# Conditional residual kernel: weight loads in runs of 2 KB with strided transposes, a smaller bias part, and row loads moved to ScalarE

## The reference

```
x: (128, 64, 256) fp32      cat_ids: (128,) in 0..63
W: (64, 256, 256) fp32      b: (64, 256) fp32
out = x + einsum('bsd,bdh->bsh', x, W[cat_ids]) + b[cat_ids][:, None, :]
```

## Time and profile before

| what | us |
|---|---|
| median of 3 runs | 99.18 |
| lowest, highest | 98.57, 100.05 |
| profiled execution, its own time | 99.0 |
| profiled execution, span | 97.0 |
| TensorE busy | 85.5 (88%) |
| VectorE, ScalarE, GpSimd busy | 53.6, 55.1, 34.3 |

### The profile page before, as it was taken

How to read it: one execution, slowest core, us unless ns; L and a number is a source line. 1 busy time by engine, 2 the same in 40 slices (tenths; PEclk the granted TensorE clock), 3 DMA queues, 4 the chain that set the end, 5 groups by cost and what they waited for, 6 DMA issues and landing times.

```text
span 97.0 us, 3027 instructions
## 1 busy us (share of the span) xinstructions
PE 85.5 (88%) x788; PEld 58.1 (60%) x788; DVE 53.6 (55%) x130; ACT 55.1 (57%) x98; POOL 34.3 (35%) x65
## 2 busy tenths in 40 slices
PE   0318969999998699999999999999999999999980
PEld 0107735676666466666767575868666866676640
DVE  2792407648236275748575475655187519664840
ACT  1402284692537282985866760977278827885500
POOL 5400000000000028999969623939702493000000
PEclk9999999999999999999999999999999999999999
DMA  0899999999999999998999999999996679999563
GB/s 13 261 345 365 348 349 346 350 346 349 350 347 349 348 350 325 341 356 267 402 367 402 365 400 370 388 388 367 329 355 252 220 171 392 409 372 343 170 209 108
DMA packets 19970, 31.25 MB, mean 322 GB/s; under 512 B 1521, under 2 KB 15986, under 8 KB 19954
## 3 DMA queue, kind: packets, MB, share of 16 engines
q0 software_dynamic: 4640, 16.26, 46.6%
q1 hardware_dynamic: 13602, 13.18, 42.3%
q10 hardware_dynamic: 1712, 1.64, 5.2%
HBM read 25.30 MB, written 8.39 MB: 347 GB/s over the span
## 4 chain that ended last, share of the span: by engine, by line
PE 62%; ACT 1%; DVE 0%; issue 0%; ACTq 0%; SPq 0%
PE mm_ps L598 42%; PE xt_ps L507 11%; PE mm_ps L584 6%; PE xt_ps L598 2%; ACT w_slot L337 1%; DVE rows L477 0%; PE xt_ps L584 0%; ACTq L337 0%; SPq L208 0%
## 5 line engine op out<-in xcount | busy, mean ns | idle before, releaser
L598 PE MATMUL mm_ps<-w_slot,xT 128*64 128x256 f32 x496 | 57.1, 380 | 2.1 <-ACT w_slot L337 2.1
L337 ACT COPY w_slot<-w_all 128x512 f32 x64 | 38.4, 619 | 28.6 <-POOLq L208 9.2
L598 PEld LDWEIGHTS mm_ps<-w_slot,xT 128*64 128x64 f32 x496 | 34.5, 137 | 19.1 <-issue 2.1
L477 DVE TENSOR_TENSOR rows<-mm_ps,rows 128x512 f32<-128x512 f32 (+1 forms) x32 | 21.6, 674 | 24.9 <-PE mm_ps L598 24.5
L337 DVE COPY w_slot<-w_all 128x512 f32 x64 | 27.2, 453 | 7.5 <-SPq L208 4.1
L192 POOL DMA_DIRECT2D w_all<-in_L_cond_W x32 | 16.4, 514 | 39.5 <-DMA w_all<-in_L_cond_W 32.2
L507 PE MATMUL xt_ps<-ident,rows 128*128 128x128 f32 x128 | 18.5, 293 | 2.3 <-DMA rows<-in_x 2.3
L349 ACT COPY xT<-xt_ps 128x512 f32<-128x512 f32 x32 | 17.2, 584 | 5.5 <-PE xt_ps L507 5.5
L507 PEld LDWEIGHTS xt_ps<-ident,rows 128*128 128x128 f32 x128 | 15.0, 150 | 7.3 <-issue 4.8
L584 PE MATMUL mm_ps<-bias_parts,is_sample 96*64 96x256 bf16 x124 | 9.9, 278 | 0.0
L223 POOL DMA_DIRECT2D out<-rows x11 | 8.7, 790 | 1.1 <-SPq L208 0.6
(11 more groups left out here) (53 smaller groups left out, 12.5 us busy)
## 6 DMA issues: line engine op xcount, KB each, us to landing
w_all<-in_L_cond_W POOLq DMA_DIRECT2D x32, 256.0 KB
w_all<-in_L_cond_W SPq DMA_DIRECT2D x29, 256.0 KB, 5.6
out<-rows POOLq DMA_DIRECT2D x11, 512.0 KB, 7.1
rows<-in_x POOLq DMA_DIRECT2D x9, 512.0 KB, 6.6
rows<-in_x SPq DMA_DIRECT2D x6, 512.0 KB, 6.6
out<-rows SPq DMA_DIRECT2D x8, 256.0 KB, 5.1
w_all<-in_L_cond_W ACTq DMA_DIRECT2D x3, 256.0 KB, 5.5
rows<-in_x ACTq DMA_DIRECT2D x1, 512.0 KB, 4.3
```

What stands on the lines that cost most here:

```text
L337: copy(w_slot[:, PAIR * p + half, :, :].rearrange("p k h -> p (k h)"), w_all[:, bass.ds(c, 1), :, :].rearrange("p c k h -> p (c k h)")).th ...
L477: V.tensor_tensor(to, sums, to, ALU.add).then_inc(sums_added, 1)
L598: last = T.matmul(to[HALF * half:HALF * (half + 1), :], xT[:, slot, k, j, :], w_slot[:, j, k, :], start=False, stop=(k == K - 1), skip_gro ...
```

## The change

- A weight matrix is read with partition p taking rows 2p and 2p+1 (one run of 2 KB in HBM) in place of rows p and 128+p (two runs of 1 KB). To fit, the transposes of x take every second column of the rows, as an operand with a step of two fp32.
- The bias table is loaded once, by SyncE. The masks are one 64x128 array, `has_category`. A tile is three products of 64 partitions and 32 columns, and all four tiles are made ahead of group 0.
- ScalarE issues x of groups 0 and 1 first, and loads 0, 4 and 7. It reads its slots (`slots_of`) for group 0 ahead of `x_half(0, ...)` and of loads 4 and 7. Later, it issues x of groups 3, 4, 5 and 6 behind its weight copies for groups 0, 1, 2 and 3. SyncE no longer issues any of these rows.
- VectorE writes `slot_words` behind the first split of the bias, and not behind all splits and masks. GpSimd's two memsets of the masks go.

```diff
-ACT_LOADS = (0, 6, 7)
+ACT_LOADS = (0, 4, 7)
-X_AFTER_LOAD = {3: 13, 4: 19, 5: 25, 6: 31, 7: 33, 8: 37, 9: 40, 10: 43, 11: 46, 12: 47, 13: 51, 14: 53, 15: 60}
+X_AFTER_LOAD = {7: 33, 8: 37, 9: 40, 10: 43, 11: 46, 12: 47, 13: 51, 14: 53, 15: 60}
+
+X_AFTER_COPIES = {0: 3, 1: 4, 2: 5, 3: 6}
...
-                             weights[bass.ds(c, 1), :, :].rearrange("c (k p) h -> p (c k) h", p=P), **how
+                             weights[bass.ds(c, 1), :, :].rearrange("c (p k) h -> p (c k) h", k=K), **how
...
-            sp.dma_start(bias_nat[0:C, :], bias).then_inc(bias_loaded, 16)
-            load_rows(sp, 0)
+            sp.dma_start(bias_nat[:, :], bias).then_inc(bias_loaded, 16)
             load_rows(sp, 2)
...
-                rows_after(sp, n)
...
-            pool.memset(in_two[:, :, :, :], 0.0).then_inc(masks_set, 1)
-            pool.memset(in_third[:, :, :, :], 0.0).then_inc(masks_set, 1)
...
-            act.dma_start(bias_nat[C:PAIR * C, :], bias).then_inc(bias_loaded, 16)
+            load_rows(act, 0)
             load_rows(act, 1)
...
+            act.wait_ge(plan_read, 2)
+            slots = slots_of(mybir.EngineType.Activation, 0, 1)
             for k in range(K):
                 x_half(0, k)
             for n in ACT_LOADS[1:]:
                 load_weights(act, n, part(word, n % WORD))
-
-            act.wait_ge(plan_read, 2)
-            slots = slots_of(mybir.EngineType.Activation, 0, 1)
...
-                    if g == 0 and p == 1:
-
-                        for k in range(K):
-                            x_half(1, k)
+                    if g == 0 and p < K:
+
+                        x_half(1, p)
+                    elif g == 0 and p == K:
+                        slots = slots_of(mybir.EngineType.Activation, 1, 1)
+                if g in X_AFTER_COPIES:
+                    load_rows(act, X_AFTER_COPIES[g])
...
+            split(V.tensor_copy(bias_first[:, :], bias_nat[:, :]))
+
             dve.wait_ge(plan_products, 4)
             V.tensor_copy(slot_words[:, :], slot_words_ps).then_inc(plan_read, 1)
+            split(V.tensor_tensor(bias_rest[:, :], bias_nat[:, :], bias_first[:, :], ALU.subtract))
+            split(V.tensor_copy(bias_second[:, :], bias_rest[:, :]))
+            V.tensor_tensor(bias_third[:, :], bias_rest[:, :], bias_second[:, :], ALU.subtract).then_inc(plan_step, 1)
+            V.tensor_scalar(has_category[:, :], mm_ps[3][0:C, 0, 0:B], iota_part[0:C, 0:1], None, ALU.is_equal
+                            ).then_inc(plan_step, 1)
...
-                    last = T.transpose(xt_ps[g % XT_SLOTS][k][:, p, :], rows[:, g % X_SLOTS, p, k * P:(k + 1) * P],
+                    last = T.transpose(xt_ps[g % XT_SLOTS][k][:, p, :], rows[:, g % X_SLOTS, p, k::K],
...
+                for n, bias_part in enumerate((bias_first, bias_second, bias_third)):
+                    last = T.matmul(bias_ps[t][TILE * n:TILE * (n + 1), :], has_category[:, TILE * t:TILE * (t + 1)],
+                                    bias_part[:, :], start=True, stop=True, skip_group_check=True)
+                return last
...
-            bias_of_tile(0).then_inc(plan_products, 1)
+            for t in range(TILES):
+                last = bias_of_tile(t)
+            last.then_inc(plan_products, 1)
...
-                    if g == 0 and pair == 0:
-
-                        for n in range(1, TILES):
-                            bias_of_tile(n).then_inc(tiles_made, 1)
```

More of the change, by code:

```diff
@@ L32 @@
 FAR = 1000.0
-PLAN_STEPS = {"samples": 6, "cats": 7, "first": 10, "list": 13, "slots": 16, "bias": 21}
-X_AFTER_LOAD = {3: 13, 4: 19, 5: 25, 6: 31, 7: 33, 8: 37, 9: 40, 10: 43, 11: 46, 12: 47, 13: 51, 14: 53, 15: 60}
+PLAN_STEPS = {"samples": 6, "cats": 7, "first": 10, "list": 13, "slots": 16, "bias": 18}
+X_AFTER_LOAD = {7: 33, 8: 37, 9: 40, 10: 43, 11: 46, 12: 47, 13: 51, 14: 53, 15: 60}
+X_AFTER_COPIES = {0: 3, 1: 4, 2: 5, 3: 6}
 STORE_AFTER_LOAD = {0: 37, 1: 40, 2: 43, 3: 46, 4: 48, 5: 51, 6: 59}
@@ L112, in build_cond_residual @@
         place_powers = sb("place_powers", [P, WORD], BF16)
-        in_two = sb("in_two", [PAIR * C, TILES, SPLITS, TILE], BF16)
-        in_third = sb("in_third", [C, TILES, SPLITS, TILE], BF16)
+        has_category = sb("has_category", [C, B], BF16)
         load_words = sb("load_words", [1, LIST_WORDS + 1], I32)
         slot_words = sb("slot_words", [1, SLOT_WORDS], I32)
-        bias_nat = sb("bias_nat", [PAIR * C, H])
-        bias_rest = sb("bias_rest", [PAIR * C, H])
-        bias_two = sb("bias_two", [PAIR * C, H], BF16)
+        bias_nat = sb("bias_nat", [C, H])
+        bias_rest = sb("bias_rest", [C, H])
+        bias_first = sb("bias_first", [C, H], BF16)
         bias_second = sb("bias_second", [C, H], BF16)
@@ L143, in build_cond_residual @@
         cat_col_ps = mm_ps[3][:, 0, B:B + 1]
-        bias_ps = [mm_ps[2 + t // PAIR][0:ROWS, t % PAIR, :] for t in range(TILES)]
+        bias_ps = [mm_ps[2 + t // PAIR][:, t % PAIR, :] for t in range(TILES)]
         cats_loaded = sem("cats_loaded")
@@ L154, in build_cond_residual @@
         plan_read = sem("plan_read")
-        masks_set = sem("masks_set")
-        tiles_made = sem("tiles_made")
         bias_step = sem("bias_step")
@@ L375, in _ @@
                 now = slots
-                if g + 1 < GROUPS:
+                if 0 < g < GROUPS - 1:
                     slots = slots_of(mybir.EngineType.Activation, g + 1, 1)
@@ L438, in _ @@
             assert steps[0] == PLAN_STEPS["slots"]
-            dve.wait_ge(bias_loaded, 32)
+            dve.wait_ge(bias_loaded, 16)
             splits = [0]
@@ L446, in split @@
                 dve.wait_ge(bias_step, splits[0])
[L448 to L464, removed]
+            split(V.tensor_copy(bias_first[:, :], bias_nat[:, :]))
             dve.wait_ge(plan_products, 4)
             V.tensor_copy(slot_words[:, :], slot_words_ps).then_inc(plan_read, 1)
+            split(V.tensor_tensor(bias_rest[:, :], bias_nat[:, :], bias_first[:, :], ALU.subtract))
[3 more added lines that the diff above has]
+                            ).then_inc(plan_step, 1)
+            steps[0] += 2
+            assert steps[0] == PLAN_STEPS["bias"]
             dve.wait_ge(plan_read, 2)
@@ L470, in put_tile @@
             def put_tile(t):
-                V.tensor_copy(bias_parts[:, t, :], bias_ps[t]).then_inc(bias_ready, 1)
+                V.tensor_copy(bias_parts[:, t, :], bias_ps[t][0:ROWS, :]).then_inc(bias_ready, 1)
             dve.wait_ge(plan_products, 5)
@@ L481, in _ @@
                 if p >= 1:
-                    dve.wait_ge(tiles_made, 1 if p == 1 else TILES - 1)
                     put_tile(p)
```

## The result

The changed kernel takes 99.97 us (median of 4 runs, 99.62 to 100.13), the kernel before 98.88 in the runs beside it. The ratio is 1.011, with a 95% interval of 1.0073 to 1.0147: slower by 1.1% where I had forecast 1.4% less. All ratios here leave out the runs that the chip disturbed; the medians in us keep them. The span of the profiled execution is 98.2 us, 1.2 more than before.

What follows compares the result with a forecast made beforehand. Weight loads bound the kernel up to group 4, TensorE after. Load 31 at 38.5 - 0.2 - 0.3 - 1.6 + 0.85 - 0.2 = 37.1 put group 4's last pair 1.4 us earlier: 97.8 us, range 95.5 to 100.3.

Steps and rivals of the forecast that it cites:

- the runs: Weight loads: runs of 2 KB cut a load from 0.753 to 0.70 us, 1.6 us over 32 loads (0 to 3.3).
- x on ScalarE's queue: Ahead of load 31: x of group 6 costs 0.85 us (0.4 to 1.5); two hardware queues give 0.2 back.
- the start: Ahead of the weights: a smaller bias table gains 0.19 us, an earlier first row load 0.3 us (0 to 0.6).
- Strided transposes: LDWEIGHTS of the transposes: a step in the operand costs 0; upper end a load of twice 0.107 us.
- rival D: Transposes of groups 6 to 15: strided loads of twice the time add 8.6 us, giving 106.4; chance 0.12, over 2% slower.
- the rule quoted under D: LDWEIGHTS: two hits to a 16-byte line hide the crossing; a two-fp32 step leaves just two, so no slowdown, without margin.
- x of groups 3 to 6: First half: x of group 6 delays load 31 by 0.85 us; a stall at group 3 falls in load time.
- The 0.2 us that two queues should give back: Before load 31: two hardware queues move 358 GB/s against 348 for one, giving back 0.2 us over 4 MB.
- Both signs of being wrong: On TensorE: LDWEIGHTS above 141 ns, or waits for x at groups 2, 5, 10 or 12 from late row loads.
- The line through the queues' packets: DMA packets: 7 ns each plus 42.5 ns per KB, so 2 KB packets take 0.93 of the time.
- rivals B and C: Weight loads: B, 2 KB runs worth twice the line, 96.1 us, chance 0.28; C, byte limit, no faster, 99.3, chance 0.15.
- The second half: From group 5 on: GpSimd's chain moves about 2 us earlier, more than TensorE's 1.4; otherwise a stall at group 12.

Runs made afterwards that it cites:

- e6: Kernel before with only the strided transposes, weights still in runs of 1 KB: 100.39 us, ratio 1.0165 to the kernel before.
- e5: Kernel before with weights in runs of 2 KB and strided transposes, nothing else of the change: 98.79 us, ratio 0.998.
- e7: Changed kernel with 1 KB weight runs, adjacent columns, and x of groups 3 to 6 issued by SyncE behind weight loads: 98.87 us, ratio 0.998 to the kernel before.
- e4: Changed kernel with weights in runs of 1 KB and transposes reading adjacent columns: 100.35 us, ratio 1.011 to the kernel before.
- e9: Kernel before with transposes reading every fourth, then every seventh column: 100.03 and 100.28 us, one run each.
- e1: Changed kernel with x of groups 3 to 6 issued by SyncE behind weight loads again: 98.51 us, ratio 0.9955 to the kernel before; repeat 98.78 us, 0.999.
- e8: Changed kernel with ScalarE issuing x of groups 3 to 6 one group earlier: 99.35 us, ratio 1.001 to the kernel before.

## Why the prediction was wrong

**The sum.** In ratios, the strided read costs 1.65% (e6), the runs of 2 KB give 1.9% (e5 against e6), the rest with x behind the loads gives 0.2% (e7), and x on ScalarE's queue costs 1.3% (e4 against e7). Together 0.85%, against a measured 1.1%, within what the intervals allow. It is a weak test, as e6 and e7 cancel in it: it says that e5 and e4 together make the change. In the forecast's own terms the strided read was 0, the runs 1.6 us gained, the start 0.5 gained and x on ScalarE's queue 0.65 lost (0.85 less 0.2). So the read is most of what the forecast missed, and x most of the rest.

**The step that failed first: "*Strided transposes.* ... I take 0".** The mechanism was rival D's, and its chance of 0.12 was for more than 2%. The load's mean duration rose from 141 to 208 ns. Measured as in the earlier trace rows, eight loads take 1.03 us in place of 0.85:

```profile
40.41 1.03 PEld L497 LDWEIGHTS xt_ps<-ident,rows 128*128 128x128 f32 x8 [0.39 <-issue]
```

That is 22 ns a load, and the transposes advance every 144 ns in place of 128, 16 ns each. It is well under D's 107, and under the 43 from which it would have decided, but over ten sets it is 1.3 us, about the size of my whole forecast. I had bounded it from both sides and written that nothing hides a slower load, and then took the lower bound for the sum with no row behind it. All that spoke for 0 was the rule quoted under D. By that rule of the Trainium skill (SBUF — State Buffer, "Door 1: The DMA port swizzle", the note on cachelines) two hits to a line suffice, so that step 2 should be free; the same note names four fp32 as the free stride. Here step 2 cost nearly what step 4 and step 7 did (e9); the measurement decides. With a unit cost that multiplies by 80 on the bound engine, the middle of the bounds, or a spread case of a few us, was due.

**The step that failed second: x of groups 3 to 6.** I priced only x of group 6, as traffic ahead of load 31, at 0.85 us, and said of group 3 that its stall would be hidden. I never followed x of groups 4 and 5, neither as traffic nor to their landing. With x of group 4 issued ahead of it, load 19 landed at 26.67 and not near 24.4 (e1). x of group 5 could not be issued before the last copy of group 2, which waits for just this load, and so went out at 26.85. It needed 8.35 us, where 1.5 us of full DMA at a third to a half share would have been 3 to 4.5. TensorE asked for it 7.1 us after the issue, less than it took. Then load 31 wasn't the gate, though it came at about the time forecast: its copy at 37.75, landing near 37.6, for 37.1. The 0.2 us that two queues should give back would be 0.3 by their own numbers (4 MB at 358 and at 348 GB/s), and it isn't there: from 15 to 25 us e4, with x on the second queue, moves 348 GB/s and e7 351.

**Right.** Both signs of being wrong that the prediction had set for these steps came: LDWEIGHTS above 141 ns, and TensorE waiting for x at group 5. The line through the queues' packets: 1.6 us for the runs, measured 1.8. A load is 262 KB / 379 GB/s = 0.69 us, for 0.70; rivals B and C fall. The rule of the Trainium skill on packet overhead (DMA: Bandwidth & Descriptors, "Why small descriptors are slow (HBM only)") gave 4% less time for a load, the line 7%, and the traces 8% (348 against 379 GB/s). The start: the first pair at 11.70 for 11.5, all tiles before 8.4 us. Group 0 ended at 17.0 for 16.3. That the start's gain is hidden behind the loads is shown by e7. The second half had no stall at groups 12 and 14, and TensorE was the bound in it.

**Not settled.** Why one or two of the 16 DMA engines end their part of a row load on the second queue some 2 us after the others, and why load 3 comes late in group 0.

## What to carry to other kernels

Before a layout is changed for the DMA's sake, multiply what it adds to one instruction of the engine that is the bound by the number of those instructions: 16 ns on 80 transposes, 1.3 us, took most of the 1.8 us that runs of 2 KB gave. A transfer that is taken from behind others on one queue and put on a second queue is bound to the time at which its engine reaches the issue, so compare issue plus a loaded landing (6.6 to 9.9 us for x of groups 3 to 6 here) with the time of its use, for every one of the transfers. It also takes from whatever it used to stand behind: load 19 took 7.4 us here in place of 4.6. Where two limits meet at one point, as loads and TensorE did in group 4, a gain on one alone shows little: the best form here that computes the result, e1, is level with the kernel before to 0.5% (0.9955 and 0.999).

## What the runs showed of the hardware that I had not expected

- A stationary fp32 operand of 128 columns with a step pays a nearly fixed price: 208 to 215 ns mean for steps of 2, 4 and 7, against 141 for adjacent elements.
- Runs of 2 KB did not give their queue more of the packets. In the changed kernel the two hardware queues moved 390 and 391 packets from 22 to 25 us (0.71 MB in mostly 2 KB packets, 0.40 MB in packets of 1 KB), and 354 and 471 from 29 to 32 us.
- One 512 KB load can be held up by one or two of its 16 DMA engines: 14 were done 6.35 us after the issue, the last after 8.35.
- In e8 the granted clock fell to half for part of a stretch, right behind waits of 0.98 and 1.65 us in group 0. Two stretches of it, with the clock in the column ahead of the DMA share:

```profile
13.50:15.50 2.00, 0.43 (x5) 0.00 (x0) 0.00 (x0) 0.62 (x1) 0.00 (x0) 1.00 1.05 390
15.50:20.00 4.50, 4.42 (x24) 2.96 (x24) 3.05 (x7) 1.86 (x3) 0.00 (x0) 0.62 1.06 388
```

A mean of 0.62 over 4.5 us is some 3.4 us at the lower of its two levels, 1.2 GHz. Sixteen products took 3.33 us there, 1.95 elsewhere.
